# Transformer block with a routed spline FFN on one core: V copied by ScalarE, output summed by three transfers

## The reference

```python
ga = (2*(ga >= 0) - 1) * maximum(abs(ga), 0.25)      # gb alike
h  = layernorm(x) * (1 + ca) + sa
# attention, one head of 256, causal:
scores = (h Wq' + bq)(h Wk' + bk)' / 16;  w = softmax(|scores| where causal)
x  = x + ga * ((w (h Wv' + bv)) Wo' + bo)
h  = layernorm(x) * (1 + cb) + sb
# FFN: 64 ternary signatures in 8 clusters; scores go through a sigmoid and an
# 8-knot line; argmax of 8 clusters, then of 8 tiles in it -> tile_idx
comp = tanh(gelu(h w1 + b1) w2 + b2)                 # 2 numbers per row
mag  = relu(comp . spline_w1[tile] + spline_b1[tile]) . spline_w2[tile] + spline_b2[tile]
y    = h + mag * directions[tile] * output_scale
out  = x + gb * (layernorm(y) * gamma + beta)
```

## Time and profile before

| | |
|---|---|
| median of 3 runs | 457.81 us (455.69 to 460.1) |
| the profiled execution | 455.52 us, its span 453.7 us |
| busy share of the span: PE, DVE, ACT, POOL | 88%, 84%, 66%, 13% |
| chain that ended last, by engine | PE 76%, DVE 12%, ACT 6%, issue 5% |
| DMA | 35.65 MB, mean 79 GB/s |

### The profile page before, as it was taken

How to read it: one execution, slowest core, us unless ns; L and a number is a source line. 1 busy time by engine, 2 the same in 40 slices (tenths; PEclk the granted TensorE clock), 3 DMA queues, 4 the chain that set the end, 5 groups by cost and what they waited for, 6 DMA issues and landing times.

```text
span 453.7 us, 7812 instructions
## 1 busy us (share of the span) xinstructions
PE 398.9 (88%) x2129; PEld 309.6 (68%) x2129; DVE 380.3 (84%) x1384; ACT 299.8 (66%) x656; POOL 58.4 (13%) x97
## 2 busy tenths in 40 slices
PE   8999999999999996999999999999999999835030
PEld 8876776877877784776877787778867777724020
DVE  3785666279698989899889989998999899998996
ACT  2246739796898594858894789569965886746020
POOL 4028311010000013020110013000220110011132
PEclk9999999999999996999999999999999999957555
DMA  8720341042103304353452305530451260015342
GB/s 241 215 53 27 121 163 46 1 116 92 25 1 116 95 32 62 61 127 116 72 93 94 116 17 113 128 94 1 71 116 47 33 109 1 1 35 82 61 63 84
DMA packets 32906, 35.65 MB, mean 79 GB/s; under 512 B 3370, under 2 KB 28448, under 8 KB 32864
## 3 DMA queue, kind: packets, MB, share of 16 engines
q1 hardware_dynamic: 24752, 26.88, 19.7%
q0 software_dynamic: 7536, 7.48, 12.2%
q10 hardware_dynamic: 576, 0.80, 0.5%
HBM read 19.36 MB, written 15.79 MB: 77 GB/s over the span
## 4 chain that ended last, share of the span: by engine, by line
PE 76%; DVE 12%; ACT 6%; issue 5%; DVEq 0%; ACTq 0%; POOL 0%; POOLq 0%
PE bank L603 14%; PE bank L620 13%; PE bank L580 12%; PE bank L593 11%; PE bank L642 6%; PE bank L611 3%; PE bank L629 3%; PE bank L568 3%; PE bank L682 2%; DVE y L2319 2%; PE bank L443 2%; DVE res L2333 1%; PE bank L673 1%; ACT L1207 1%; DVE sp L2277 1%
## 5 line engine op out<-in xcount | busy, mean ns | idle before, releaser
L620 PE MATMUL bank<-v,probsT 128*128 128x257 f32 x320 | 79.5, 382 | 1.5 <-ACT probsT L1284 1.0
L603 PE MATMUL bank<-h,g 128*128 128x128 f32 (+3 forms) x256 | 78.2, 436 | 1.3 <-ACT gath L1356 0.8
L593 PE MATMUL bank<-m_ga,h 128*128 128x258 f32 x256 | 66.2, 384 | 0.8 <-DVE negmax L2148 0.8
L620 PEld LDWEIGHTS bank<-v,probsT 128*128 128x128 f32 x320 | 57.6, 190 | 12.1 <-issue 2.6
L580 PE MATMUL bank<-h,a_sb 128*128 128x512 f32 x128 | 62.1, 609 | 3.7 <-DVE cmp_t L2268 3.7
L593 PEld LDWEIGHTS bank<-m_ga,h 128*128 128x128 f32 x256 | 46.3, 192 | 13.2 <-issue 6.3
L603 PEld LDWEIGHTS bank<-h,g 128*128 128x128 f32 x256 | 42.8, 190 | 17.7 <-issue 9.3
L2035 POOL DMA_DIRECT2D out<-res x14 | 18.1, 1295 | 279.8 <-DVE res L2333 279.8
L2148 DVE CUSTOM_DVE_ANT_0 probs<-bank,cmask 128x128 f32<-128x128 f32 (+1 forms) x64 | 31.0, 484 | 18.1 <-ACT bank L1273 17.8
L1266 ACT ACTIVATE g<-bank,g_bias 128x512 f32<-128x512 f32 x32 | 21.9, 688 | 33.0 <-PE bank L580 32.9
L1273 ACT ACTIVATE bank<-bank,v 128x128 f32<-128x128 f32 (+1 forms) x64 | 31.6, 500 | 11.9 <-PE bank L603 10.5
(11 more groups left out here) (183 smaller groups left out, 808.6 us busy)
## 6 DMA issues: line engine op xcount, KB each, us to landing
x<-in_L_attn_x SPq DMA_DIRECT2D x16, 512.0 KB, 4.0
out<-x SPq DMA_DIRECT2D x14, 512.0 KB, 4.9
out<-res POOLq DMA_DIRECT2D x14, 512.0 KB, 6.4
gb_row<-gate_rows SPq DMA_DIRECT2D x16, 256.0 KB, 3.5
a_row<-gate_rows SPq DMA_DIRECT2D x14, 256.0 KB, 3.3
out<-res SPq DMA_DIRECT2D x2, 512.0 KB, 3.6
wide<-in_L_wmod SPq DMA_DIRECT2D x1, 768.0 KB, 11.9
wide<-in_L_wmod ACTq DMA_DIRECT2D x1, 512.0 KB, 5.8
```

The source lines that it names most:

```text
L593: last = mm(ps[:, 0:VW], h[s][:, c, t * P:(t + 1) * P], m_ga[p % 2][s][:, c, :], start=(c == 0), stop=(c == KC - 1))
L603: last = mm(ps[:, 0:w], g[s][:, c, t * P:(t + 1) * P], h[s][:, c, 0:w], start=(c == 0), stop=(c == KC - 1))
L620: last = mm(ps[:, 0:D + 1], probsT[s][t][:, j * P:(j + 1) * P], v_sb[s][:, j, 0:D + 1], start=(j == 0), stop=(j == t))
```

## The change

The lists of all engines and the bank table are written anew. By part:

- **Values.** From pair 1 on `b_v` moves to ACT as a plain copy out of PSUM (56 tiles). The bias column is now column 0 of V (`TCOL = 0, VAL = 1`), the ones column is set once, and a new small DVE instruction, `b_tc`, adds the constant of the score bias into `tc`, which `b_abs` takes. The first pair's tiles keep the add on DVE. V's matmul has 257 columns instead of 258.
- **The value-bias row** is added to x itself: POOL issues an accumulating transfer `bx` that adds the gated row, from DRAM, to all 512 rows of an image in `x_sb`, once `xhat` has been made. `b_x2` waits for it.
- **Output of groups 0 to 6.** SP writes the gated beta row to all 512 rows of `out` (`beta`, DRAM to DRAM, instead of `xo`); POOL then accumulates x2 (`ax`) and later y (`ay`). `oa` and `ob` give way to ACT's `yh` (y * rstd + nmr) and DVE's `yg` (times the gamma row). y has two buffers, and `y_` of group g waits for `ay` of group g - 2. Groups 7 and 8 keep `oa` and `ob`.
- **Gated matrices** (`ms`) and `base` move from POOL to DVE.
- **Loads.** The gate part of `wmod` moves from ACT's queue to SP's, behind a wait for the first part; `ldga` loads one row instead of two; `ldga` and `ldgb` wait for the new last readers. The warm-up of PE around the transpose of c is cut from 8 and 16 calls to 4 and 9, and `su_ga` stands behind the first two V tiles. Small setup tiles lie in the second y buffer.

```diff
-    ONE, TCOL = D, D + 1
+    TCOL, VAL, ONE = 0, 1, D + 1
...
+            spq.wait_ge(in_mod, 16)
+            load(in_mod_ga, wmod_sb[:, :, 2 * D:3 * D], wmod_v[:, :, 2 * D:3 * D])
             weight(in_o, wo, "Wo")
...
-            def xo(g, i):
+            def beta(g, i):
                 p, s = of_group(g, i)
-                spq.wait_ge(x2_rdy, NT * (before(g) + i + 1))
-                spq.dma_start(out_v[GROUPS[g][i]], x2[p % 2][s][:, :, :]).then_inc(x2_sent[p % 2][s], 16)
...
+                need(spq, x2_sent[p % 2][s], 16 * (p // 2))
+                rows_ = gate_rows[GROUPS[g][i]:GROUPS[g][i] + 1, 3 * D:4 * D]
+                spq.dma_start(out[GROUPS[g][i]], rows_.broadcast_to([S, D])).then_inc(beta_sent[p % 2][s], 16)
...
-                busy(BUSY_BANK, 16)
+                busy(BUSY_BANK, 9)
...
+            def b_v(p, s, t):
+                b = seq(p, s)
+                act.wait_ge(v_done, NT * b + t + 1)
+                if t == 0:
+                    need(act, pv_done, prev(p, s))
+                need(act, tc_rdy, NT * (seq(p - 1, s) - 2) + t + 1 if p > 1 else 0)
+                A(v_sb[s][:, t, 0:ONE], banks[BANK[f"V{s}{t}"]][:, 0:ONE], ACT.Identity).then_inc(v_ready, 1)
...
+            def bx(p, s):
...
+                pool.wait_ge(xhat_ready, NT * b + NT - XHAT_DVE)
+                row = gate_rows[b:b + 1, D:2 * D].unsqueeze(1).broadcast_to([P, NT, D])
+                gp.dma_start(x_sb[p % 2][s][:, :, :], row, accum_op=ALU.add).then_inc(x_summed[p % 2][s], 16)
...
+            def ax(g, i):
...
+                pool.wait_ge(beta_sent[p % 2][s], 16 * (p // 2 + 1))
+                pool.wait_ge(x2_rdy, NT * (before(g) + i + 1))
+                gp.dma_start(out_v[GROUPS[g][i]], x2[p % 2][s][:, :, :], accum_op=ALU.add).then_inc(x2_sent[p % 2][s], 16)
...
             def ay(g, i):
...
-                pool.wait_ge(alone_rdy, NT * (before(g) + i + 1))
+                pool.wait_ge(scaled_rdy, NT * (before(g) + i + 1))
...
+            def b_tc(p, s, t):
+                b = seq(p, s)
+                dve.wait_ge(v_ready, NT * (b - 2) + t + 1)
...
+                ts(tc[s][:, t:t + 1], v_sb[s][:, t, TCOL:TCOL + 1], a_row[0][0][:, D:D + 1], None,
+                   ALU.add).then_inc(tc_rdy, 1)
...
             def b_x2(p, s, t):
...
+                need(dve, x_summed[p % 2][s], 16 * ((p + 1) // 2))
...
             def y_(g, t):
...
-                need(dve, alone_rdy, min(NT * before(g), NT * before(g - 1) + t + 1))
+                need(dve, summed[g % 2][t // NT], 16 * (g // 2))
...
+            def yg(g, t):
+                dve.wait_ge(yhat_rdy, NT * before(g) + t + 1)
...
+                own = y[g % 2][:, t, :]
+                tt(own, own, gb_row[g % 2][t // NT][:, 0, :], ALU.mult).then_inc(scaled_rdy, 1)
```

More of the change, by code:

```diff
@@ L2070, in _ @@
-            ay(6, 1)
-            for i in range(0, 2):
-                base(8, i)
+                ay(6, i)
         @block.vector
@@ new lines, in _ @@
+            for i in range(1, 3):
+                a_st(4, 1, i)
+            lob(1, 0)
+            b_ri(3, 0, 0)
+            for i in range(1, 4):
+                lob(1, i)
+            a_st(4, 1, 3)
+            b_tc(3, 1, 0)
+            a_var(4, 0)
+            y_st(0, 3)
+            lob(1, 4)
+            b_x2(3, 0, 0)
+            oh(1, 0)
+            a_var(4, 1)
+            oh(1, 1)
+            ms(4, 1)
+            for i in range(2, 4):
+                a_var(4, i)
+            ms(5, 0)
@@ new lines, in _ @@
+            b_ttr(3, 1, 3)
+            for i in range(0, 2):
+                pick(2, i)
+            y_nw(0, 1)
+            spl(1, 0)
+            b_st(3, 0, 3)
+            b_st(3, 1, 0)
+            spl(1, 1)
+            b_ri(3, 1, 1)
+            spl(1, 2)
+            y_nw(0, 2)
+            spl(1, 3)
+            y_nw(0, 3)
+            b_x2(3, 1, 1)
+            for i in range(4, 6):
+                spl(1, i)
+            loc(2, 0)
+            y_(1, 0)
+            loc(2, 1)
+            b_tc(4, 0, 0)
@@ new lines, in _ @@
+            y_st(3, 7)
+            b_ttr(6, 0, 3)
+            b_tc(6, 1, 0)
+            a_nw(7, 1)
+            b_ri(6, 0, 0)
+            b_x2(6, 0, 0)
+            for i in range(2, 4):
+                yg(2, i)
+            b_st(6, 0, 0)
+            b_ttr(6, 1, 0)
+            clc(5, 0)
+            b_tc(6, 1, 1)
+            y_var(3, 0)
+            a_nw(7, 2)
+            clc(5, 1)
+            b_tc(6, 1, 2)
+            clc(5, 2)
+            y_var(3, 1)
+            clc(5, 3)
+            y_var(3, 2)
@@ L3354, in _ @@
[L3354 to L3361 removed]
+            c_b2(5)
+            yg(3, 3)
+            y_st(4, 2)
+            for i in range(2, 4):
+                c_nw(6, i)
+            loc(5, 4)
+            b_tc(7, 0, 3)
+            y_st(4, 3)
+            for i in range(5, 7):
+                y_(4, i)
+            loc(5, 5)
+            y_st(4, 4)
@@ new lines, in _ @@
+            b_tc(7, 1, 0)
+            b_st(7, 0, 0)
+            b_ri(7, 0, 1)
+            lob(5, 3)
+            b_x2(7, 0, 1)
+            lob(5, 4)
+            for i in range(0, 2):
+                y_nw(4, i)
+            b_ttr(7, 0, 3)
+            b_tc(7, 1, 1)
+            y_nw(4, 2)
+            oh(5, 0)
+            y_nw(4, 3)
+            oh(5, 1)
+            b_st(7, 0, 1)
+            yg(3, 7)
+            for i in range(0, 7):
+                clc(6, i)
+            b_ttr(7, 1, 0)
@@ new lines, in _ @@
+            for i in range(7, 10):
+                clc(6, i)
+            b_ttr(7, 1, 1)
+            clb(6, 0)
+            b_ri(7, 0, 2)
+            clb(6, 1)
+            b_x2(7, 0, 2)
+            for i in range(2, 5):
+                clb(6, i)
+            pick(6, 0)
+            b_st(7, 0, 2)
+            pick(6, 1)
+            b_tc(7, 1, 2)
+            b_ri(7, 0, 3)
+            yg(4, 0)
+            b_x2(7, 0, 3)
+            spl(5, 0)
+            b_st(7, 0, 3)
+            spl(5, 1)
```

3680 lines of the change are left out of this document (1825 added, 1855 removed), and 16 rows, old and new, of the table BANK.

## The result

The change made the kernel slower: 479.12 us median (474.24 to 483.77, 4 runs) against 458.28 us.

What follows compares the result with a forecast made beforehand. PE was taken to set the pace from 21.5 to 394 us, DVE after that. 455.5 - 7.0 (dense stretch) - 9.0 (tail) - 1.5 (start) = 438.0, with 2.3 to the median 440.3: forecast 440, range 427 to 456.

Steps and rivals of the forecast that it cites:

- Transfers: POOL's 42 transfers instead of 14, engines at some 55% with SP's queue: landings covered by margins, priced at nothing.
- Who waits: DVE's waits for the new transfers: y_ for ay with margins of 2 and 0.7 us, b_x2 for bx; priced at nothing.
- The first rival: Accumulating transfers land late, past 7 to 8.5 us, and DVE waits for them: 471 us, chance 0.12.
- POOL's arithmetic leaves: Dense stretch, 21.5 to 394 us: POOL no longer holds DVE, PE's hole at 170 us closes; -7.0 us, bounds -11.1 and 0.
- DVE's account: Dense stretch: DVE's busy time falls by about 35 of 315.6 us, as slack and no term of its own.
- The tail: After PE's last attention product: DVE has 9.0 us less to do; term -9, bounds -11 and -4.
- The start: Setup: shorter PE warm-up and su_ga behind the first V, but later loads; -1.5 us, bounds -3 and +4.
- ACT "is covered": Dense stretch: with its added work ACT needs 20.1 to 20.9 us per image against PE's 22.6, so no cost.
- The second rival: ACT becomes the bound of the dense stretch, at 23.9 us per image instead of 22.6: 458 us, chance 0.15.

Runs made afterwards that it cites:

- e3: The changed kernel without the bx transfers and with x2 sent plainly by SP in place of beta and ax; 448.1 us.
- e11: The changed kernel with bx and beta reading 512 different rows of the input, beta's in separate 1 KB pieces; 452.3 us.
- e7: The kernel before the change with only the gated matrices of pairs 2 to 7 moved from POOL to DVE; 450.9 us.
- e9: e7 with ACT's yh, one DVE product per tile, beta and ax for groups 5 and 6 alone, beta behind the last x load; 450.1 us.
- e5: e3 also without ACT's 56 normalisations yh, y left unnormalised; 445.7 us.
- e2: The changed kernel with x2 sent plainly by SP in place of beta and ax, bx kept; 463.2 us.
- e12: The complete changed kernel with both rows first written four times to DRAM, so bx and beta read 4 KB 128 times; 453.8 us.

## Why the prediction was wrong

- **The step that failed is *Transfers*.** It priced `bx` as one more accumulating transfer of 6.4 us and put `beta` between 3.5 and 9.8 us, "so neither end shows"; together with the waits it priced the new transfers at nothing. They cost 27 us (475.3 less e3's 448.1). With little company `bx` and `beta` take some 10 us, and 23 of the 27 go when they read other rows (e11). The share of the engines that it worked out, 55%, was right (0.55 in the dense stretch); the time of one transfer was not. No row of before reads one row of DRAM 512 times: the broadcast gate rows take 3.5 us, but repeat a stretch of 2 KB 128 times. The bound for `bx` should have been as wide as that for `beta`.
- **"Who waits" named the wrong waiter.** It listed those that wait for the new transfers (`y_`, `b_x2`): these lost 4.4 and 2.4 us. The 34.7 us fell on the x loads, which share the engines with the new transfers and are triggered by the same `b_x2` as `ax`. Their cover, some 0.5 to 11 us, is thinner at its low end than any margin that the prediction listed (7.1 us and more), and the prediction did not work it out.
- **The first rival** had the sign and nearly the size (471 us, 0.12), with margins of the wrong transfers, so its nearness is luck. Its point of decision, a landing past 7 to 8.5 us, was passed by `bx`, `ax` and `beta`, but not by `ay` (6.5). The rule it cites gets no support: POOL's issues of `ay` still take 1.29 us, and `bx` lands 3.6 us sooner (8.3 instead of 11.9) when only the place it reads changes.
- **POOL's arithmetic leaves: right.** No DVE instruction takes over 1 us in the dense stretch any more, and e7 gives the 7.0 alone. DVE's account of that stretch was too large, -24 us (315.6 to 291.4 in e3) for -35, but the prediction hung no term on it.
- **The tail: in its bounds** (-6.5 in e3, 59.7 to 53.2, for -9). DVE's work there fell by the 9.0 forecast (54.2 to 45.2). But in e9 less work alone did not shorten the tail: it takes 5.9 us off DVE in the old order, with `base` still on POOL, and gains nothing. Whether the new order or the move of `base` makes the difference, no run separates.
- **The start: right** (first G matmul 20.3 in e3, 21.5 before, -1.2 for -1.5).
- **ACT "is covered": not quite.** The sum without its transfers, 440, met 448 in e3; the dense gain of 7 was given back, and PE's longest waits there are on ACT's `onehotT` (3.1 us) and `probsT` (2.5). The second rival's mechanism holds at most for part of it (e5).

## What to carry to other kernels

Before adding transfers, list the loads that are already there and the time between the event that frees their buffer and their first use: in this kernel the tightest of these paid, whoever issued the new traffic. Price a transfer by a row with the same source pattern, not only the same bytes; here the broadcast of one small DRAM row over a whole tile was worth a few copies of that row (21.5 us for 128 KB). And take a bundle apart: one part alone (12 instructions from POOL to DVE) carried some 7 of the 10 us that the bundle gives without its transfers.

## What the runs showed of the hardware

- 512 KB made from one DRAM row of 1 KB, read 512 times, landed in 9.5 us accumulating into SBUF (e2) and 9.1 from DRAM to DRAM (changed kernel), each with only a row load of 128 KB beside it; made from one stretch of 4 KB, read 128 times, in 5.0 and 5.2 (e12). Beside all other traffic the medians are 11.9 and 11.3 from the one row, 8.3 and 6.8 from 512 different rows in as many packets (e11), 7.7 and 7.1 from the stretch of 4 KB (e12).
- The share of the engines hardly shows it: the queue of POOL holds 34.2% of 16 engines' span in the changed kernel and 32.9% in e11, 23 us faster.
- In the changed kernel a 512 KB x load issued 1 to 7 us behind another 512 KB transfer landed in 8.6 to 12.6 us (eight loads), the others in 3.7 to 6.2 (four).
- A POOL tensor_tensor that reads SBUF held DVE instructions up to its own end; with the twelve large ones of the dense stretch gone, the granted clock there is 1.00 instead of 0.99 and the hole is closed (e7).
